# The sweep stage of a metaformer block: PE's loop over steps written out, and the late wait stated first

## The chip, the cores and the metric

One core of a Trainium2 chip runs the whole program. The metric is the device time of one execution in microseconds, median of the runs. Engines: PE (matmul; PEld is its weight load), DVE (vector), ACT (scalar), POOL (GpSimd), SP (which issues most DMAs).

## What is computed

The input is `x`, 8 images of 32 channels, 64 by 64, f32. Two blocks follow each other, each with a residual mixer and a residual mixture of experts. The first mixer is a spectral convolution. The second, which the change touches, is four dependent sweeps over the image's rows or columns:

```python
def _sweep(x, w, b, axis, reverse):
    rows = jnp.moveaxis(x, axis, 0)
    if reverse:
        rows = rows[::-1]
    def step(prev, row):
        new = row + jax.nn.relu(_conv1d(prev, w, b))
        return (new, new)
    _, rest = jax.lax.scan(step, rows[0], rows[1:])
    ...

out = _sweep(x, w_d, b_d, axis=2, reverse=False)
out = _sweep(out, w_u, b_u, axis=2, reverse=True)
out = _sweep(out, w_r, b_r, axis=3, reverse=False)
out = _sweep(out, w_l, b_l, axis=3, reverse=True)
```

`_conv1d` is a 9-tap convolution along the row with 32 channels in and out. A sweep has 64 rows, so 63 steps; four sweeps have 252 steps, and each step needs the one before it.

## The kernel before

The program is written engine by engine, with semaphores between them; each engine runs its own list in order. Ahead of the sweeps lie the first block (layer norm, spectral convolution, experts) and the second layer norm; behind them the second experts (`experts(1)`) and the store.

**A row in memory.** The partition holds 4 neighbouring pixels times 32 channels (128), the free dimension 8 images times 16 groups of pixels. The 9 taps become 3 banded matrices of 128 by 128 (`conv_sb`), one for each neighbouring group. The current row stands in `state`, in RE, a ring of 4 slots with padding at both ends.

**Three chains.** The 8 images are split in three (`CHAINS`: 3, 3 and 2), so that one chain's matmuls run while the others are with DVE. For each step and chain PE (L718) runs 3 taps times 4 column strips of 32 (`OC`), 12 matmuls of 128 rows by 32 columns over 48 or 32 values. They are f32, and each gives two recorded passes, so a step is 36 matmuls or 72 passes. They accumulate on a bias that ACT wrote into the PSUM bank beforehand (`seed`, L851; two seeds a step, for chains 0 and 1 together and for chain 2). DVE (L1111) then takes the ReLU, adds the input row and writes the new state in one operation for each chain. POOL (L392), in the fourth sweep ACT (L865), copies the finished row to the image (the archive).

**Semaphores.** `s_st` counts the states that DVE wrote, `s_seed` the seeds, `s_cv` the convolutions that PE finished, `s_arc` and `s_arl` the archived rows. PE waits ahead of each chain for the state of the last step, and ahead of chains 0 and 2 also for the seed. DVE waits ahead of each chain for `s_cv`, and once a step for the archive of four rows back, so that a state slot is free.

**Loops.** For each of the four sweeps, PE's code has three steps written out (`u` from 1 to 3 of group 0) and then a hardware loop, `pe.Fori(1, HO)`, of 15 turns with 4 steps each. The loop's waits compare with values that registers hold and that are counted up. DVE, ACT and POOL have all 252 steps written out with constants. Ahead of sweep 3 and during sweeps 2 and 4, DMAs move rows and columns between layouts (`move_rows`, L317; `move_columns`, L328).

Of the kernel before, what the change touches and what calls it, by code (L numbers as in the profile page):

```python
# [8 lines left out]
B, C, H, W = 8, 32, 64, 64  # L9
# [5 lines left out]
Q = 4  # L15
HO = H // Q
# [6 lines left out]
CHAINS = ((0, 3), (3, 6), (6, 8))  # L23
# [17 lines left out]
def build_kernel(nc, x_in, dft, wspec, conv_w, conv_b, gate_w, gate_b, w1, w2, b2, own, out):  # L41
# [5 lines left out]
    with ExitStack() as ctx:  # L47
# [3 lines left out]
        def sem(name):  # L51
            return ctx.enter_context(nc.semaphore(name))
# [63 lines left out]
        s_st, s_cv = sem("state_ready"), sem("conv_ready")  # L116
        s_seed, s_arc, s_pad = sem("bias_in_bank"), sem("row_archived"), sem("state_zeroed")
        s_bits, s_arl = sem("banks_written"), sem("last_rows_archived")
# [139 lines left out]
        def row_count(s, t):  # L258

            return 127 * (s // 2) + 63 * (s % 2) + t + 1  # L260

        def state_count(s, t, c):

            return len(CHAINS) * (row_count(s, t) - 1) + c + 1

        def seed_of(c):

            return next(i for i, (c0, c1) in enumerate(SEEDS) if c0 <= c < c1)

        def state_slot(s, u):  # L270

            return (u + 3 * (s % 2)) % 4

        def conv_bank(s, u, c):

            b0, b1 = CHAINS[c]
            c0, c1 = SEEDS[seed_of(c)]
            bank = 2 * c0 + (s + u + 1) % 2 * (c1 - c0) + c - c0
            return PS[:, bank, 0:(b1 - b0) * HO].rearrange("p (b v) -> p b v", v=HO)
# [6 lines left out]
        def row_at(image, s, q, u):  # L286

            if s % 2:
                q, u = HO - 1 - q, Q - 1 - u
            if image is XF:  # L290
                return XF[:, Q * q + u]
            if image is XW:
                return XW[:, u, :, q, :]
            return XV[:, u, :, :, q]
# [8 lines left out]
        def wait_columns(eng, j):  # L303

            share = sum(on_pool(j, i) for i in range(Q))
            eng.wait_ge(s_ph[j], 16 * (Q * len(MOVED) - share))
            eng.wait_ge(s_php[j], 16 * share)
# [102 lines left out]
        def _(pe):  # L410
# [298 lines left out]
            for s in range(4):  # L709
                def step(q, u):  # L710
                    for c, (b0, b1) in enumerate(CHAINS):
                        if c == SEEDS[seed_of(c)][0]:
                            pe.wait_ge(s_seed, len(SEEDS) * (63 * s + Q * q + u - 1) + seed_of(c) + 1)
                        pe.wait_ge(s_st, state_count(s, Q * q + u - 1, c))
                        for d in range(3):
                            prev = state[:, state_slot(s, u - 1), b0:b1, d:d + HO]
                            for o in range(0, P, OC):
                                m = pe.matmul(conv_bank(s, u, c)[o:o + OC], conv_sb[:, s, d, o:o + OC], prev,  # L718
                                              start=False, stop=(d == 2), skip_group_check=True)
                        m.then_inc(s_cv, 1)  # L720

                for u in range(1, Q):
                    step(0, u)
                with pe.Fori(1, HO) as q:
                    for u in range(Q):
                        step(q, u)

            experts(1)

# [144 lines left out]
        def _(dve):  # L874
# [216 lines left out]
            for s in range(4):  # L1091
                if s % 2 == 0:
                    if s == 0:
                        dve.wait_ge(s_pad, 1)
                        dve.wait_ge(s_fd, 16)
                    else:
                        wait_columns(dve, 0)
                    for b0, b1 in CHAINS:
                        dve.tensor_copy(state[:, 0, b0:b1, 1:1 + HO], row_at(SRC[s], s, 0, 0)[:, b0:b1, :]).then_inc(s_st, 1)
                else:  # L1100
                    dve.wait_ge(s_arc, 63 * (s - 1) + 62)

                def step(q, u):
                    r = Q * q + u
                    if s == 3 and r > Q:
                        dve.wait_ge(s_arl, r - Q)
                    elif 63 * s + r > Q:
                        dve.wait_ge(s_arc, 63 * s + r - Q)
                    for c, (b0, b1) in enumerate(CHAINS):
                        dve.wait_ge(s_cv, len(CHAINS) * (63 * s + Q * q + u - 1) + c + 1)  # L1110
                        dve.scalar_tensor_tensor(out=state[:, state_slot(s, u), b0:b1, 1:1 + HO], in0=conv_bank(s, u, c),  # L1111
                                                 scalar=0.0, in1=row_at(SRC[s], s, q, u)[:, b0:b1, :],
                                                 op0=ALU.max, op1=ALU.add).then_inc(s_st, 1)

                for r in range(1, H):
                    if s == 2 and r < Q:
                        wait_columns(dve, r)
                    step(r // Q, r % Q)
# [71 lines left out]
```

## Time and profile before

| | us |
|---|---|
| median of 3 runs | 687.14 |
| lowest and highest | 681.44, 689.34 |
| the profiled execution | 681.41 |
| its span, first to last instruction | 679.6 |
| PE busy | 589.5 (87%) |
| DVE busy | 393.8 (58%) |
| ACT busy | 318.2 (47%) |
| POOL busy | 99.3 (15%) |
| mean granted clock of TensorE | 0.935 |

All prediction sums are made against the profiled execution. The sweeps' first matmul starts 293.9 us into the span, and their last ends at about 584 us. "Released by issue" means that the engine waited for nothing that the profile shows. PE's busy time counts pipelined passes with modelled ends. Queues named "instruction" bring program code to the engines.

### The profile page before, as it was taken

What the parts mean: (1) busy time and instruction counts of PE and PEld (TensorE: products, weight loads), DVE (VectorE), ACT (ScalarE), POOL (GpSimd) and SP (SyncE); (2) the same over time, 40 slices, a digit from 0 to 9 for tenths busy, and PEclk for the clock granted to TensorE, in tenths of its full rate; (3) what the DMA queues carried; (4) which work ended last, traced back from release to release, by engine and by line L of the source; (5) the groups of instructions that cost most, each with busy time, mean ns of one, the idle gap of its engine ahead of it and who ended that gap; (6) DMA issues with size and microseconds to landing.
All of it is one profiled execution on the core that took longest, in us unless ns stands there. A gap on an engine that the chain in (4) does not pass through costs nothing.

```text
span 679.6 us, 47989 instructions
## 1 busy us (share of the span) xinstructions
PE 589.5 (87%) x21958; PEld 542.8 (80%) x21958; DVE 393.8 (58%) x1077; ACT 318.2 (47%) x842; POOL 99.3 (15%) x220
## 2 busy tenths in 40 slices
PE   8978898999979999869997899679996999965897
PEld 7978788999969869858887888568885888964783
DVE  4648896574498265624554455436663555388626
ACT  4757896533584023433443343314443666548600
POOL 4000000000110000012222222412220033620000
PEclk9989899999988799988998899969999999987979
DMA  9631770500000000000000032310000233300006
GB/s 361 256 124 64 291 270 3 215 34 1 1 1 2 18 1 0 1 3 2 0 0 2 2 78 78 78 19 1 0 0 4 44 66 65 67 9 1 2 2 247
DMA packets 54411, 41.01 MB, mean 60 GB/s; under 512 B 49350, under 2 KB 49478, under 8 KB 53126
## 3 DMA queue, kind: packets, MB, share of 16 engines
q1 hardware_dynamic: 53816, 39.29, 18.0%
q8 instruction: 46, 0.75, 0.5%
q0 software_dynamic: 384, 0.39, 0.3%
q10 hardware_dynamic: 144, 0.39, 0.2%
q14 instruction: 21, 0.17, 0.1%
HBM read 27.49 MB, written 4.19 MB: 47 GB/s over the span
## 4 chain that ended last, share of the span: by engine, by line
PE 63%; DVE 17%; ACT 6%; SPq 6%; issue 5%; DMA 1%; POOL 0%; DVEq 0%; ACTq 0%
PE PS L718 29%; PE PS L434 5%; PE PS L687 4%; SPq L328 4%; DVE RB L958 4%; PE PS L455 3%; DVE RE L1111 3%; PE PS L509 2%; SPq L317 2%; DVE sums L997 2%; PE PS L637 2%; DVE RCD L1009 2%; PE PS L584 2%; PE PS L533 2%; PE PS L540 2%
## 5 line engine op out<-in xcount | busy, mean ns | idle before, releaser
L718 PE MATMUL PS<-RE,conv_sb 128*32 128x48 f32 (+1 forms) x18144 | 248.2, 209 | 42.2 <-issue 17.0
L718 PEld LDWEIGHTS PS<-RE,conv_sb 128*32 128x32 f32 x18144 | 231.6, 114 | 58.8 <-issue 26.8
L851 ACT COPY PS<-convb_sb 128x96 f32<-128x96 f32 x504 | 106.7, 215 | 169.0 <-DVE RE L1111 161.4
L1111 DVE SCALAR_TENSOR_TENSOR RE<-PS,RCD 128x48 f32<-128x48 f32 x378 | 74.2, 203 | 68.6 <-PE PS L718 55.0
L392 POOL COPY RCD<-RE 128x128 f32<-128x128 f32 x126 | 37.0, 293 | 206.4 <-DVE RE L1111 206.4
L1111 DVE SCALAR_TENSOR_TENSOR RE<-PS,RE 128x48 f32<-128x48 f32 x189 | 39.0, 223 | 32.5 <-PE PS L718 23.5
L1111 DVE SCALAR_TENSOR_TENSOR RE<-PS,RB 128x48 f32<-128x48 f32 x189 | 37.1, 203 | 33.6 <-PE PS L718 26.6
L784 ACT COPY RB<-PS 32x256 f32<-32x256 f32 x64 | 42.5, 664 | 7.3 <-PE PS L493 6.5
L958 DVE COPY RB<-PS 32x256 f32<-32x256 f32 x64 | 42.1, 658 | 5.6 <-PE PS L493 4.8
L455 PE MATMUL PS<-warm 128*128 128x128 bf16 x468 | 38.3, 255 | 6.2 <-ACT RCD L824 3.6
L455 PEld LDWEIGHTS PS<-warm 128*128 128x128 bf16 x468 | 35.3, 117 | 7.4 <-ACT RCD L824 4.0
L509 PE MATMUL PS<-RE,RB 128*64 128x64 f32 x1024 | 32.7, 225 | 8.2 <-DVE RCD L967 4.0
L509 PEld LDWEIGHTS PS<-RE,RB 128*64 128x64 f32 x1024 | 31.5, 140 | 9.6 <-DVE RB L958 5.3
L884 DVE TENSOR_REDUCE sums<-RE 128x32 f32<-128x1024 f32 x16 | 19.4, 1218 | 33.2 <-ACT RE L756 33.2
L756 ACT ACTIVATE RE<-PS 128x1024 f32<-128x1024 f32 x16 | 16.2, 1021 | 33.6 <-PE PS L434 33.5
L385 POOL TENSOR_TENSOR RE<-RA 128x1024 f32<-128x1024 f32 x3 | 5.7, 1893 | 179.5 <-ACT RA L817 179.5
L434 PEld LDWEIGHTS PS<-dft_sb,RCD 128*128 128x128 f32 x128 | 30.5, 328 | 0.9 <-issue 0.5
L687 PE MATMUL PS<-RCD,espread 128*128 128x512 f32 x64 | 31.2, 644 | 0.0
L434 PE MATMUL PS<-dft_sb,RCD 128*128 128x128 f32 x128 | 30.8, 396 | 0.0
L745 ACT COPY RCD<-PS 128x256 f32<-128x256 f32 (+1 forms) x40 | 24.7, 692 | 11.2 <-PE PS L698 6.0
L803 ACT COPY RB<-PS 128x512 f32<-128x512 f32 (+1 forms) x24 | 16.2, 736 | 26.1 <-PE PS L540 26.1
L614 PE MATMUL PS<-proj,RA 128*128 128x192 f32 x128 | 23.4, 343 | 5.6 <-ACT RB L817 5.2
(117 smaller groups left out, 780.8 us busy)
## 6 DMA issues: line engine op xcount, KB each, us to landing
RE<-wspec SPq DMA_DIRECT2D x8, 2048.0 KB, 8.5
RA<-x_in SPq DMA_DIRECT2D x8, 512.0 KB, 7.4
RCD<-x_in SPq DMA_DIRECT2D x1, 4096.0 KB, 13.6
out<-RA SPq DMA_DIRECT2D x8, 512.0 KB, 2.7
RCD<-RB SPq DMA_DIRECT2D x48, 64.0 KB, 2.1
RE<-RCD SPq DMA_DIRECT2D x32, 80.0 KB
RE<-RCD SPq DMA_DIRECT2D x16, 64.0 KB
RCD<-RB SPq DMA_DIRECT2D x26, 32.0 KB, 1.9
```

The source lines that it names most:

```text
L328: eng.dma_start(CO[C * bl:C * bl + C, k, i, w0:w0 + Q * (v1 - v0)], XF[C * i:C * i + C, Q * v0:Q * v1, BH * bl:BH * bl + BH, :]).then_inc( ...
L392: pool.tensor_copy(o, i).then_inc(s_arc, 1)
L434: m = pe.matmul(blk(ln_slot(g), n), src, centre, start=True, stop=True)
L455: pe.matmul(PS[:, bank, 0:P], warm[:, :], warm[:, :], start=True, stop=True)
L509: m = pe.matmul(o[:, x % 2, y], XB[:, c % 2, x, 2 * y + a].rearrange("p r q b -> p (r q b)"), WR[:, c % 3, a, x, y, :], start=True, stop=True)
L687: pe.matmul(PS[:, 4 + k % 4, :], espread[:, BL * bh:BL * bh + BL, :].rearrange("p b o -> p (b o)"), rhs, start=True, stop=True).then_inc(s ...
L718: m = pe.matmul(conv_bank(s, u, c)[o:o + OC], conv_sb[:, s, d, o:o + OC], prev, start=False, stop=(d == 2), skip_group_check=True)
L745: m = act.copy(o, i)
L784: m = act.copy(o, i)
L851: act.copy(banks_of, convb_sb[:, s:s + 1].unsqueeze(2).to_broadcast([P, c1 - c0, n])).then_inc(s_seed, 1)
L958: m = dve.tensor_copy(o, i)
L1111: dve.scalar_tensor_tensor(out=state[:, state_slot(s, u), b0:b1, 1:1 + HO], in0=conv_bank(s, u, c), scalar=0.0, in1=row_at(SRC[s], s, q, u ...
```

## The change

On PE, the three steps written out and the loop of 15 turns give way to one Python loop that writes out all 63 steps of each sweep; every wait then compares with a constant. Ahead of chains 0 and 2 PE states its wait for `s_st` before that for `s_seed`. On DVE the archive's wait, which stood ahead of the step's chains, now stands behind chain 0's wait for `s_cv`. The matmuls, vector operations and DMAs are the same in number, shape and order.

```diff
--- before.py
+++ after.py
@@ -709,9 +709,9 @@
             for s in range(4):
                 def step(q, u):
                     for c, (b0, b1) in enumerate(CHAINS):
+                        pe.wait_ge(s_st, state_count(s, Q * q + u - 1, c))
                         if c == SEEDS[seed_of(c)][0]:
                             pe.wait_ge(s_seed, len(SEEDS) * (63 * s + Q * q + u - 1) + seed_of(c) + 1)
-                        pe.wait_ge(s_st, state_count(s, Q * q + u - 1, c))
                         for d in range(3):
                             prev = state[:, state_slot(s, u - 1), b0:b1, d:d + HO]
                             for o in range(0, P, OC):
@@ -719,11 +719,8 @@
                                               start=False, stop=(d == 2), skip_group_check=True)
                         m.then_inc(s_cv, 1)
 
-                for u in range(1, Q):
-                    step(0, u)
-                with pe.Fori(1, HO) as q:
-                    for u in range(Q):
-                        step(q, u)
+                for r in range(1, H):
+                    step(r // Q, r % Q)
 
             experts(1)
 
@@ -1101,13 +1098,13 @@
                     dve.wait_ge(s_arc, 63 * (s - 1) + 62)
 
                 def step(q, u):
-                    r = Q * q + u
-                    if s == 3 and r > Q:
-                        dve.wait_ge(s_arl, r - Q)
-                    elif 63 * s + r > Q:
-                        dve.wait_ge(s_arc, 63 * s + r - Q)
                     for c, (b0, b1) in enumerate(CHAINS):
-                        dve.wait_ge(s_cv, len(CHAINS) * (63 * s + Q * q + u - 1) + c + 1)
+                        r = Q * q + u
+                        dve.wait_ge(s_cv, len(CHAINS) * (63 * s + r - 1) + c + 1)
+                        if c == 0 and s == 3 and r > Q:
+                            dve.wait_ge(s_arl, r - Q)
+                        elif c == 0 and 63 * s + r > Q:
+                            dve.wait_ge(s_arc, 63 * s + r - Q)
                         dve.scalar_tensor_tensor(out=state[:, state_slot(s, u), b0:b1, 1:1 + HO], in0=conv_bank(s, u, c),
                                                  scalar=0.0, in1=row_at(SRC[s], s, q, u)[:, b0:b1, :],
                                                  op0=ALU.max, op1=ALU.add).then_inc(s_st, 1)
```

## Rows read from the trace of the kernel before

**Rows 1.** The page's part 1: busy us, share of the span, instructions.

```profile
PE 589.5 (87%) x21958; PEld 542.8 (80%) x21958; DVE 393.8 (58%) x1077; ACT 318.2 (47%) x842; POOL 99.3 (15%) x220
```

**Rows 2.** The page's part 5: busy, mean ns, then idle before and releaser.

```profile
L718 PE MATMUL PS<-RE,conv_sb 128*32 128x48 f32 (+1 forms) x18144 | 248.2, 209 | 42.2 <-issue 17.0
```

**Rows 3.** Stretches: length, then busy us and instructions by engine, clock, DMA share.

```profile
365.80:378.30 12.50, 8.23 (x471) 7.33 (x460) 4.09 (x21) 2.71 (x13) 1.76 (x6) 0.68 0.02 5
378.30:436.30 58.00, 53.69 (x4032) 50.32 (x4032) 32.97 (x169) 23.72 (x113) 16.42 (x56) 0.98 0.23 57
526.20:584.20 58.00, 53.37 (x4032) 49.66 (x4032) 33.12 (x169) 36.09 (x166) 15.48 (x6) 1.00 0.35 59
sum 290.30, PE 248.17 PEld 231.63 DVE 150.75 ACT 120.72 POOL 74.95; mean PE 31.02 PEld 28.95 DVE 18.84 ACT 15.09 POOL 9.37
```

**Rows 4.** Time line: start, length, group, idle before it; DVE's sweep operations.

```profile
344.57 0.66 DVE L1111 SCALAR_TENSOR_TENSOR RE<-PS,RCD 128x48 f32<-128x48 f32 x3 [0.25 <-PE PS L718]
345.85 0.66 DVE L1111 SCALAR_TENSOR_TENSOR RE<-PS,RCD 128x48 f32<-128x48 f32 x3 [0.63 <-PE PS L718]
346.74 0.66 DVE L1111 SCALAR_TENSOR_TENSOR RE<-PS,RCD 128x48 f32<-128x48 f32 x3 [0.23 <-PE PS L718]
```

**Rows 5.** Chain of waits in order of time: start, length, what.

```profile
344.50 0.02 DVEq L1110
```

**Rows 6.** Time line, PE alone, start of sweep 1.

```profile
298.14 1.90 PE L718 MATMUL PS<-RE,conv_sb 128*32 128x32 f32 x124 [1.68 <-issue]
302.18 2.45 PE L718 MATMUL PS<-RE,conv_sb 128*32 128x48 f32 x123 [2.14 <-issue]
306.15 1.19 PE L718 MATMUL PS<-RE,conv_sb 128*32 128x48 f32 x55 [1.53 <-issue]
```

**Rows 7.** Time line, PE alone, start of sweep 2.

```profile
369.49 2.42 PE L718 MATMUL PS<-RE,conv_sb 128*32 128x32 f32 x123 [1.61 <-issue]
373.12 2.45 PE L718 MATMUL PS<-RE,conv_sb 128*32 128x48 f32 x124 [1.20 <-issue]
376.80 5.91 PE L718 MATMUL PS<-RE,conv_sb 128*32 128x48 f32 x349 [1.23 <-issue]
```

**Rows 8.** Time line, PE alone, start of sweep 3.

```profile
441.91 1.51 PE L718 MATMUL PS<-RE,conv_sb 128*32 128x48 f32 x72 [6.01 <-DVE RE L1099]
450.71 2.23 PE L718 MATMUL PS<-RE,conv_sb 128*32 128x48 f32 x123 [0.70 <-issue]
454.62 1.05 PE L718 MATMUL PS<-RE,conv_sb 128*32 128x48 f32 x68 [1.68 <-issue]
```

**Rows 9.** Time line, PE alone, start of sweep 4.

```profile
517.39 1.98 PE L718 MATMUL PS<-RE,conv_sb 128*32 128x48 f32 x124 [1.61 <-issue]
521.19 1.84 PE L718 MATMUL PS<-RE,conv_sb 128*32 128x48 f32 x124 [1.82 <-issue]
524.86 1.24 PE L718 MATMUL PS<-RE,conv_sb 128*32 128x32 f32 x73 [1.82 <-issue]
```

**Rows 10.** Queues (packets, MB, share): whole span; 366 to 379 us; 319 to 366 us.

```profile
q8 instruction: 46, 0.75, 0.5%
...
q8 instruction: 4, 0.07, 2.0%
...
q14 instruction: 3, 0.02, 0.2%
```

**Rows 11.** Stretches: half clock in sweep 1, the mix, a burst in sweep 4.

```profile
306.15:312.10 5.95, 5.78 (x311) 5.65 (x314) 2.44 (x12) 1.72 (x8) 1.09 (x4) 0.50 0.01 3
72.20:78.70 6.50, 4.59 (x127) 4.38 (x127) 6.23 (x10) 5.99 (x10) 0.00 (x0) 1.00 0.66 277
536.20:546.80 10.60, 9.78 (x744) 9.12 (x743) 6.17 (x33) 6.64 (x32) 0.00 (x0) 1.00 0.59 99
```

**Rows 12.** Time line, PE alone, in the spectral mix.

```profile
72.24 0.94 PE L493 MATMUL PS<-dft_sb,RA 128*128 128x128 f32 x7 [0.92 <-issue]
78.76 0.45 PE L509 MATMUL PS<-RE,RB 128*64 128x64 f32 x8 [1.93 <-issue]
```

## The prediction

> **What bounds the kernel now.** I read the page's busy shares first. PE works 87% of a span of 679.6 us, and 18,144 of its 21,958 recorded passes are one line, L718, the three-chain sweep [rows 1, 2]. Then I cut the sweeps' 290.3 us (293.9 to 584.2) into stretches [rows 3]. They fall into two kinds. Each sweep begins with code that runs once (three peeled steps, then the first turn of the loop, 7 steps or 504 passes), and goes on with 14 more turns of the same loop code (56 steps, 4,032 passes). The repeated part takes 58.0 us for 56 steps in sweep 2, 1.04 us a step. Sweep 2's first-run part takes 12.5 us for 7 steps, 1.79 us a step, for the same matmuls. What the unrolled program will resemble is this first-run part, because all its code is run once. So the question is what makes it slow.
>
> In the repeated part, the time line shows DVE's bursts of three at 344.57, 345.85 and 346.74 [rows 4]: a step of 1.28 us over the turn of the loop, and one of 0.89 us within it, where PE is nearly full (72 passes). With 0.9 us for a plain step, the turn costs 0.38 us. In the chain of waits, DVE's queue stands at L1110 at 344.50, 0.02 us long, and DVE's operation begins at 344.57 [rows 4, 5]: the wait for PE, stated last of two, is taken as an instruction of its own and costs some 0.06 us.
>
> In the first-run parts PE stops for 0.70 to 2.14 us with the releaser "issue", which means that nothing the profile shows was awaited: no semaphore, no data [rows 6 to 9]. Between two such stops stand 123 or 124 passes each time. A pass is two instructions (weight load and matmul), so that is 248 instructions and a few waits and register operations. The queue that carries code fits this exactly. Queue q8 moved 46 packets, 0.75 MB, 16 KB each [rows 10]. Counting each sweep's loop body once, PE's program has (21,958 - 18,144 + 4 x 7 x 72) x 2 = 11,660 instructions and a few waits, 253 or more a packet: 64 bytes each, a packet being a page of 256. Around the first-run part of sweep 2, from 366 to 379 us, q8 moves 4 packets, and in the 47 us of repeated loop from 319 to 366 us none at all, only another engine's q14 appears [rows 10]. So loops run from code already on the chip, and straight code is fetched page by page, each page arriving when the previous one has long been used up.
>
> **The page period.** From resumption to resumption the seven intervals are 4.04 and 3.97 (sweep 1), 3.63 and 3.68 (sweep 2), 3.91 (sweep 3), 3.80 and 3.67 us (sweep 4) [rows 6 to 9]; mean 3.81. In each of them PE needs 1.8 to 2.5 us from first to last pass and then starves. That it starves three times running, without the gap shrinking, says that the fetch is one page ahead only and does not build up a lead. Four packets in 13 us is of the same size.
>
> **The change, part by part.**
> (a) Removed: 60 loop turns, with their register operations and branches. In the loop regime this would save 60 x 0.38 = 22.8 us [rows 4]. Under a page period of 3.81 us it saves nothing, for a page's own work is far shorter: 256 instructions at 146 a step are 1.75 steps, 1.6 us at 0.9 us a step. Even at a granted clock of 0.50 (the lower level, 1.2 GHz), where 311 passes or 4.3 steps take 5.95 us [rows 11], it is 1.75 x 1.38 = 2.4 us. So the clock, which was 0.68 in the starved stretch of sweep 2 [rows 3], doesn't enter the sum.
> (b) Added: straight code. A step is 72 passes x 2 = 144 instructions and two extra waits (two of the three chains have two waits, of which one needs its own instruction), 146. 252 steps x 146 / 256 = 143.7 pages. At 3.81 us: 547.5 us. Bounds: 3.63 gives 521.6, 4.04 gives 580.5.
> (c) Columns at the start of sweep 3: PE waited 6.01 us for the first state [rows 8], and then briefly for the next columns. A fetch under way there covers some of it; a page's period at most (3.8), half of it on average: + 5 us with the later waits (0 to 7).
> (d) Transfers in the sweeps. Sweeps 2 and 4 have bursts of rows and columns being moved; the DMA share is 0.23 and 0.35 over the 58 us of repeated loop [rows 3], and 0.59 within the burst from 536.2 [rows 11]. So the bursts run (0.23 + 0.35) x 58 / 0.59 = 57 us in all; their work stays the same. No page was fetched in them, so the price is not shown. The nearest row is the spectral mix, where the DMA share is 0.66 and PE resumes after "issue" at 72.24 and 78.76: a period of 6.52 us [rows 11, 12], of which its own passes take 4.6. At 6.52 us the bursts hold 57 / 6.52 = 9 pages, each 2.7 us late, 24 us; at the quiet period it is 0. I take 12, the middle, as the share is near the mix's but the code before the stop was slower there.
> (e) The DVE's late wait first: 0.02 + 0.04 us less before DVE's first chain, at most 0.06 x 60 turns = 4 us on today's path (within a turn PE is the bound), and 0 behind a page fetch. The same holds for PE's swapped order of `s_st` and `s_seed`: mostly, both semaphores are up when the page comes. Bounds: 0 to -4.
> (f) Everything outside the sweeps: unchanged, 0 (up to 2 more if the next stage starts at half clock).
>
> Sum: 547.5 + 5 + 12 = 564.5 us in place of 290.3, + 274. The profiled execution took 681.41 us (span 679.6), so 681.4 + 274 = **955 us**. That execution is at the fast end of the three runs (681.44 to 689.34, median 687.14), and an after held by fetches should scatter no less; I leave 955. By the bounds: 681.4 + (521.6 - 290.3) - 4 = 909, and 681.4 + (580.5 + 7 + 24 - 290.3) + 2 = 1,005.
>
> A rule speaks against this. The Trainium skill (Runtime: NRT & Kernel Launch, section "Instruction fetch mechanics") says that the sequencer streams straight code by itself, that crossing a 16 KiB boundary is mostly hidden, and that kernels prefer full unrolling over branches. The trace disagrees: thirteen crossings cost 0.70 to 2.14 us each [rows 6 to 9, 12].
>
> **The rivals.**
> 1. Faster. The stops are a start-up matter, of the first pages after a loop, and once straight code runs on, the fetch keeps up. Place: each 256-instruction boundary in L718. Price: the turns go (-22.8), the late waits too (-4), and if the first-run parts fall to 7 x 0.9 = 6.3 us as well, 6.2 in each of four sweeps (-25): 630 to 659 us, about 650. It decides once the page period is under 1.75 x 1.04 = 1.8 us. For it: crossings elsewhere go unnoticed. Against: those codes take over 4 us a page by themselves, with 128-column matmuls, and the same stop appears in the mix at 72.24 and 78.76, which no loop precedes [rows 12]. 0.06. The skill's rule above would give this outcome.
> 2. No change. Two pages in flight, a period of half 3.81: 143.7 x 1.91 = 274 us and the columns' 5, 670 to 690 us. Against: q8 shows one packet per period. 0.02.
> 3. Slower, by less. The period measured is partly that of pages entered behind a loop or beside the profiler, and runs at about 3.0 us: 143.7 x 3.0 = 431, 681.4 + 431 + 17 - 290.3 = 839; 760 to 905. 0.10.
> 4. Slower still. The small packets of the moves hold back fetches more than in the mix, or the quiet period is over 4.04: over 1,010 us. 0.10.
> 5. The change doesn't do what it says, because the builder keeps a loop: excluded, the steps are written out one by one.
>
> **The numbers.** My forecast (909 to 1,005) has 0.72, rivals 1 to 4 0.06, 0.02, 0.10 and 0.10. Predicted time 955 us, range 895 to 1,015: the forecast's own 0.72 and the near edges of rivals 3 and 4, together some 0.8. A measurement of this kernel can tell about 1% from no change. Faster by over 1% 0.06, within 1% 0.02, slower 0.92.
>
> **What would show it.** q8 should move 46 + (252 x 146 - 4 x 1,036) / 256 = 173 packets, about 2.8 MB, spread evenly over the sweeps, 3.6 to 4.1 us apart (1,036 is a sweep's code now). The waits should show L718 "issue" as the largest entry, some 140 times, with runs of 123 to 125 passes between. PE's busy share should fall to about 0.6 or less, the sweeps' slices to tenths of 4 to 6. DVE's bursts should come in irregular steps, mean 2.2 us, and its wait at L1110 should leave the chain. My prediction is wrong if the pages arrive closer than 3 us (then the lead does build up), or if DVE or PE at half clock rather than "issue" ends most stops. The share of (d) shows as a longer period inside the bursts.

## The result and the profile after

The changed kernel takes 946.78 us (median of 4 runs, 942.8 to 952.64) beside 688.0 us before: a ratio of 1.380, 95% interval 1.369 to 1.391. That is slower by 259 us, with 955 us forecast and a range of 895 to 1,015. The profiled execution took 950.65 us (span 948.8), 269.2 us more than that of before; the sum had said 274. The kernel before has shorter and longer executions (676 to 693 us in all groups), and every ratio compares the shorter ones of both kernels, so that it can differ from the quotient of the medians.

The page of the changed kernel, parts 1 and 2 (busy time and share; tenths of busy time in 40 slices of 23.7 us), the code queue of part 3, and PE's sweep line of part 5:

```profile
PE 651.4 (69%) x21958; PEld 598.8 (63%) x21958; DVE 399.7 (42%) x1077; ACT 315.8 (33%) x842; POOL 100.4 (11%) x220
...
PE   8888899979996565555454655556555544569698
...
PEclk9999999998996856867868557775766889759758
...
q8 instruction: 174, 2.85, 1.3%
...
L718 PE MATMUL PS<-RE,conv_sb 128*32 128x48 f32 (+1 forms) x18144 | 305.5, 240 | 252.4 <-issue 245.8
```

These answer to [rows 1, 2, 10]. The number of passes is the same. Their idle time went from 42.2 to 252.4 us, and 245.8 us of it has the releaser "issue" (17.0 before). The code queue moved 174 packets in place of 46; 173 had been worked out. The middle slices, all of the sweeps, are half busy.

PE's waits over the whole span (engine, line, releaser, us in total, times, longest):

```profile
PE PS L718 <- issue: 245.8, 141, 2.8
```

That is one stop a page: 141 for 143.7 pages. And the time line of PE in sweep 1 (start, length, passes, idle time before):

```profile
307.21 2.56 PE L718 MATMUL PS<-RE,conv_sb 128*32 128x48 f32 x126 [1.15 <-issue]
310.71 2.59 PE L718 MATMUL PS<-RE,conv_sb 128*32 128x32 f32 x127 [0.95 <-issue]
314.67 1.59 PE L718 MATMUL PS<-RE,conv_sb 128*32 128x48 f32 x126 [1.38 <-issue]
318.58 1.66 PE L718 MATMUL PS<-RE,conv_sb 128*32 128x48 f32 x126 [2.31 <-issue]
322.18 1.58 PE L718 MATMUL PS<-RE,conv_sb 128*32 128x48 f32 x126 [1.95 <-issue]
326.11 1.66 PE L718 MATMUL PS<-RE,conv_sb 128*32 128x32 f32 x127 [2.34 <-issue]
```

It is the pattern of [rows 6 to 9], now without end: 126 or 127 passes, then a stop (123 to 125 had been expected; with the few waits between them they make 256 instructions). Read the starts, not the lengths. A page's work takes 1.6 us or 2.6 us, and the stop before the next page is mostly the shorter, the longer the work was, so that the starts stand 3.50 to 3.96 us apart all the same. A cost that came with each page would be added to its work; a period covers the work.

What the period is made of can be read from the code queue between two such starts, 318.58 and 322.18 (40 slices of 0.09 us; a packet's bytes stand in the slice in which it starts):

```profile
GB/s 0 0 0 0 0 0 0 0 0 0 0 0 182 0 0 0 0 0 0 0 0 0 0 0 0 0 0 0 0 0 0 0 0 0 0 0 0 0 0 0
q8 instruction: 1, 0.02, 1.8%
```

The one packet starts at 319.71, 1.1 us after PE has entered the page, ends at 320.78, and PE enters the next page 1.4 us behind that. The trace has it so in every one of the 139 periods of the sweeps that can be cut out: one packet, starting 1.34 us (mean; 1.06 to 2.25) after PE enters a page, 1.15 us long, and the next page entered 1.39 us (1.19 to 1.61) after its end. So a page is asked for when PE enters the one before it, and not earlier: that is what "one page ahead" means here.

By stretch (length, then busy us and instructions of PE, PEld, DVE, ACT and POOL, granted clock, DMA share, GB/s), one line for each sweep:

```profile
291.40:423.00 131.60, 76.52 (x4495) 71.09 (x4495) 37.93 (x187) 26.69 (x128) 18.19 (x62) 0.69 0.02 5
423.00:565.00 142.00, 77.01 (x4545) 71.61 (x4545) 38.33 (x189) 26.43 (x126) 18.48 (x63) 0.69 0.12 30
565.00:707.00 142.00, 78.69 (x4544) 72.96 (x4545) 42.15 (x193) 26.11 (x126) 22.51 (x70) 0.68 0.04 8
707.00:849.50 142.50, 73.24 (x4560) 67.99 (x4559) 38.59 (x191) 40.08 (x186) 17.28 (x7) 0.75 0.18 30
sum 558.10, PE 305.45 PEld 283.65 DVE 157.00 ACT 119.31 POOL 76.46; mean PE 76.36 PEld 70.91 DVE 39.25 ACT 29.83 POOL 19.11
```

The sweeps take 558.1 us in place of 290.3, so 267.8 of the 269.2 us are theirs. The part ahead of them is 2.5 us shorter (291.4 in place of 293.9), the part behind them 3.9 us longer.

### The profile page after: what moved, and what is told of

It is laid out like the page before. It is cut to its first block, busy times and chain, and to the rows that moved or that the text cites. A ratio compares the mean times of both kernels' runs of the same rounds, so it can differ in the third digit from the quotient of the medians.

```text
span 948.8 us, 47145 instructions
## 1 busy us (share of the span) xinstructions
PE 651.4 (69%) x21958; PEld 598.8 (63%) x21958; DVE 399.7 (42%) x1077; ACT 315.8 (33%) x842; POOL 100.4 (11%) x220
## 4 chain that ended last, share of the span: by engine, by line
PE 56%; issue 27%; DVE 12%; ACT 3%; SPq 1%; POOL 1%; DMA 0%; ACTq 0%
PE PS L718 32%; PE PS L434 4%; PE PS L687 3%; DVE RB L955 3%; PE PS L637 2%; DVE sums L994 2%; DVE RCD L1006 2%; PE PS L584 2%; PE PS L533 1%; PE PS L455 1%; PE PS L540 1%; PE PS L614 1%; PE PS L509 1%; PE PS L554 1%; DVE RCD L1029 1%
## 5 line engine op out<-in xcount | busy, mean ns | idle before, releaser
L718 PE MATMUL PS<-RE,conv_sb 128*32 128x48 f32 (+1 forms) x18144 | 305.5, 240 | 252.4 <-issue 245.8
L718 PEld LDWEIGHTS PS<-RE,conv_sb 128*32 128x32 f32 x18144 | 283.7, 139 | 274.3 <-issue 267.7
L1108 DVE SCALAR_TENSOR_TENSOR RE<-PS,RCD 128x48 f32<-128x48 f32 x378 | 76.7, 203 | 199.5 <-PE PS L718 185.6
L1108 DVE SCALAR_TENSOR_TENSOR RE<-PS,RE 128x48 f32<-128x48 f32 x189 | 41.6, 223 | 95.8 <-PE PS L718 85.6
L1108 DVE SCALAR_TENSOR_TENSOR RE<-PS,RB 128x48 f32<-128x48 f32 x189 | 38.3, 203 | 102.7 <-PE PS L718 95.6
L881 DVE TENSOR_REDUCE sums<-RE 128x32 f32<-128x1024 f32 x16 | 19.4, 1218 | 34.0 <-ACT RE L753 34.0
L392 POOL COPY RB<-RE 128x128 f32<-128x128 f32 x63 | 18.5, 293 | 118.5 <-DVE RE L1108 118.5
L334 POOL TENSOR_TENSOR RA<-RCD 128x1024 f32<-128x1024 f32 x6 | 17.0, 2853 | 106.2 <-DMA RCD<-RB 106.2
L994 DVE TENSOR_REDUCE sums<-RE 128x32 f32<-128x1024 f32 x16 | 19.4, 1213 | 16.1 <-ACT RE L812 11.0
```

The lines of the kernel that those rows point to most:

```text
L392: pool.tensor_copy(o, i).then_inc(s_arc, 1)
L994: dve.tensor_reduce(sums[:, 32 * g:32 * g + 32], square[:, g % 2, 0:1024].rearrange("p (a c) -> p a c", c=C), AX_X, ALU.add).then_inc(s_su ...
```

## The experiments

Theory: straight code reaches PE in pages of 256 instructions, one page ahead, one every 3.8 us or so; code of a loop stays on the chip. The rivals: the waits (their order, or constants in place of registers), the granted clock, a fixed cost a page or a step, and the size of what stays on the chip. The kernel before ran beside all of them; its median was 683.0 to 687.8 us in the three groups. Where no ratio stands, medians are compared.

**The order of the waits alone.**

```diff
 PE, in the loop, which stays
-                        if c == SEEDS[seed_of(c)][0]:
-                            pe.wait_ge(s_seed, ...)
                         pe.wait_ge(s_st, state_count(s, Q * q + u - 1, c))
+                        if c == SEEDS[seed_of(c)][0]:
+                            pe.wait_ge(s_seed, ...)
 DVE: as in the change
```

> The kernel before with the order of the two waits changed on PE and DVE and nothing else; PE keeps its loop. Theory (code pages: a page of 256 instructions arrives every 3.87 us, one ahead, and only straight code pays): no page is added, so 684 to 688 us beside a before of 688: a gain of at most 60 turns x 0.06 = 4 us. Rival (the slowdown comes from the way the waits are taken): a visible part of the 259 us shows here, over 700.

Measured: 686.87 us beside 686.4, ratio 1.013 (1.007 to 1.019). The medians are level and the ratio lies on the slow side: the swap brings nothing, and costs two hundredths at most (13 us by the interval). By this run it has at most a twentieth of the 259 us. The chain of waits in the repeated part of sweep 1, of this kernel:

```profile
341.45 3.47 PE PS L718 x264
344.92 0.02 issue
344.94 0.22 DVE RE L1111
345.17 0.02 issue
345.19 0.25 ACT PS L851
345.44 0.02 issue
345.46 3.45 PE PS L718 x264
```

DVE's queue at L1110 [rows 5] is out of the chain, as the change meant, but a turn of the loop still takes 4.01 us (341.45 to 345.46), against 4.04 at the same place before (341.22 to 345.26). At most 0.03 of the 0.06 us show.

**The unrolling alone.**

```diff
 PE, waits in their old order; DVE as before
-                for u in range(1, Q):
-                    step(0, u)
-                with pe.Fori(1, HO) as q:
-                    for u in range(Q):
-                        step(q, u)
+                for r in range(1, H):
+                    step(r // Q, r % Q)
```

> The kernel before with PE's sweep program written out over 63 steps a sweep, waits in their old order on both engines. Page theory: 940 to 955, as with the whole change, 174 packets on the code queue and some 140 stops with the releaser issue. Rival (wait order matters in straight code): differs from 947 by over 10 us, to either side.

Measured: 941.79 us beside 686.4, ratio 1.388 (1.380 to 1.397). Its code queue and PE's wait at L718:

```profile
q8 instruction: 174, 2.85, 1.3%
...
PE PS L718 <- issue: 207.1, 139, 2.6
```

The whole loss is the unrolling's: its 255 us are the 259 of the whole change, within the scatter of runs. This profile also speaks against the granted clock as the cause. The mean clock was 0.750 here and 0.795 in the changed kernel, and PE was busy for 682.1 us in place of 651.4. Yet the execution was not longer (944.20 us, against 950.65), because the stops are shorter in sum, 207.1 us in place of 245.8.

**More steps in a loop turn.** Three sizes of the loop's body, each with all 63 steps of a sweep:

```diff
 12 steps a turn (20: the same with 5 in place of 3, and 3 turns)
-                with pe.Fori(1, HO) as q:
-                    for u in range(Q):
-                        step(q, u)
+                with pe.Fori(0, 5) as g:
+                    for j in range(3):
+                        for u in range(Q):
+                            step(3 * g + (j + 1), u)
 8 steps a turn
-                for u in range(1, Q):
-                    step(0, u)
-                with pe.Fori(1, HO) as q:
-                    for u in range(Q):
-                        step(q, u)
+                for r in range(1, 8):
+                    step(r // Q, r % Q)
+                with pe.Fori(1, 8) as g:
+                    for j in range(2):
+                        for u in range(Q):
+                            step(2 * g + j, u)
```

> The kernel before with 12 steps in a loop turn and 5 turns, in place of 4 steps and 15 turns. The loop's code is 12 x 150 = 1,800 instructions, 7.0 pages. Page theory, if the chip holds 7 pages: first-run code grows from 7 to 15 steps a sweep, 4.7 pages x 4 sweeps x (3.87 - 1.8) = + 39 us, 40 turns fewer are - 15 us: about 712 us, with 46 + 4 x 4.7 = 65 code packets. Rival (nothing but the branch counts, straight code is free): 688 - 15 = 673. Rival (what is held is smaller than 7 pages): every turn is fetched anew, 930 or more and 170 or more packets.

> The kernel before with 20 steps in a loop turn and 3 turns; the loop's code is 20 x 150 = 3,000 instructions, 11.7 pages. Page theory with a store of less than 11 pages on the chip: all of it is fetched in each turn, 940 to 990 us and 170 or more code packets, although there is a loop. If the store holds it: first-run code is 23 steps a sweep, 9.4 pages more x 4 x 2.07 = + 78, turns - 18: about 748 us with 84 packets.

> The kernel before with 7 steps written out and then 7 loop turns of 8 steps; the loop's code is some 1,197 instructions, 4.7 pages. Page theory with a store of about 8 pages on the chip (a turn of 7.0 pages was held in one sweep and fetched anew in another): this one is always held. First-run code is 15 steps a sweep, 8.7 pages in place of 4.1: 4.6 x 4 x (3.81 - 1.8) = + 37 us, 32 turns fewer - 12: about 713 us, 64 code packets. Rival (what is held is below 4.7 pages): 900 or more and over 150 packets. Rival (straight code costs nothing, turns do): 676.

Measured: 12 steps 923.48 us beside 686.4; 20 steps 999.77 beside 686.4, ratio 1.476 (1.468 to 1.484); 8 steps 713.23 beside 683.03, ratio 1.052 (1.044 to 1.061). The code queue tells them apart. With 20 steps a turn, over the whole span and from 393 to 440 us, about one turn:

```profile
q8 instruction: 189, 3.10, 1.3%
...
q8 instruction: 13, 0.21, 1.9%
```

A body of 11.7 pages is fetched anew in each turn, loop or no loop, and costs even more than straight code. With 12 steps a turn, the whole span, then 425 to 456 us (one turn of sweep 2), then 338 to 361 us (two turns of sweep 1):

```profile
q8 instruction: 155, 2.54, 1.2%
...
q8 instruction: 8, 0.13, 1.7%
...
q14 instruction: 2, 0.02, 0.2%
```

The same 7.0 pages were held in three turns of sweep 1 and fetched anew in every turn of sweep 2. By my expectation it should have been one or the other throughout. Over the four sweeps, six of the 16 repeated turns ran without a stop, three each in sweeps 1 and 4, and ten were fetched anew. The time line of PE in sweep 4 shows one turn of each kind, one behind the other:

```profile
769.09 11.28 PE L718 MATMUL PS<-RE,conv_sb 128*32 128x48 f32 x864 [0.47 <-ACT PS L852]
785.67 1.97 PE L718 MATMUL PS<-RE,conv_sb 128*32 128x48 f32 x93 [5.30 <-issue]
788.85 2.45 PE L718 MATMUL PS<-RE,conv_sb 128*32 128x48 f32 x123 [1.21 <-issue]
```

A held turn is 864 passes without a stop; a missed one begins with a stop of 5.30 us here (3.82 at 429.22, in sweep 2), which I take for the price of a branch to code that isn't there, and goes on page by page. So 7.0 pages are on the edge. What decides between the two, these runs don't show. With 8 steps a turn, 4.7 pages, the whole span, and then 291 to 320 us:

```profile
q8 instruction: 65, 1.06, 0.6%
...
q8 instruction: 8, 0.13, 1.9%
```

From 320 to 353 us no packet of q8 appears at all, in 2,280 passes. And the time is 30 us over the kernel before, where 25 had been worked out: the turns saved are less than the first-run code added. (That the 713 us came out to the microsecond is luck, as the kernel before was 5 us quicker in this group.) The Trainium skill (Runtime: NRT & Kernel Launch, section "Instruction fetch mechanics") gives PE an instruction store of 128 KiB, 2,048 instructions, which is 8 pages. The three runs agree in size, with 4.7 pages held and 11.7 not; but the 7.0 pages, which are under 8, were missed in most turns.

**Fewer instructions for the same arithmetic.** A strip of 64 or 128 columns halves or quarters the code of a step:

```diff
-OC = P // 4
+OC = P // 2      (or P)
```

> The kernel before with two column strips of 64 per tap in place of four of 32: 72 instructions a step in place of 144, same arithmetic. In the mix a pass of 64 columns and 64 values takes 3.95 us / 128 = 31 ns, so 48 values some 23 ns and a step 36 x 23 ns = 0.83 us, near the 0.9 of now. Page theory: the first-run code of a sweep falls from 4.1 to 2.2 pages, whose own work is then as long as a fetch, so some 4 x 6 = 24 us go: about 664 (645 to 690). Rival (strips of 64 make PE slower than the code saves): over 690.

> The changed kernel (all steps written out) with strips of 64: 74 instructions a step, 72.8 pages. Page theory: 72.8 x 3.87 = 282 us for the sweeps, 5 for the columns, so 681 + 287 - 290 = 678 (665 to 700), and the code queue falls from 174 to 103 packets, with a period of still some 3.9 us for 256 instructions. Rival (straight steps cost 2.2 us each by their waits or by the clock, not by their bytes): still about 945. Rival (a gap per page, not a period: 1.7 us a page whatever the page's own work): 252 x 0.9 + 72.8 x 1.7 = 351, so 742.

Measured: with the loop 668.44 us beside 687.81, ratio 0.974 (0.959 to 0.990); unrolled 694.24 beside 687.81. Queues of the unrolled kernel, whole span and 300 to 420 us; its sweeps; PE's waits in them; two stops in its PE time line; and the sweeps of its partner with the loop:

```profile
q8 instruction: 103, 1.69, 1.0%
...
q8 instruction: 31, 0.51, 1.9%
...
295.00:588.00 293.00, 276.67 (x9070) 272.08 (x9070) 157.11 (x757) 121.86 (x564) 74.84 (x202) 0.98 0.15 30
...
PE PS L718 <- issue: 6.3, 19, 0.6
...
392.92 3.85 PE L718 MATMUL PS<-RE,conv_sb 128*64 128x48 f32 x124 [0.58 <-issue]
397.42 2.77 PE L718 MATMUL PS<-RE,conv_sb 128*64 128x48 f32 x88 [0.65 <-issue]
```

```profile
291.00:572.00 281.00, 274.51 (x9072) 273.43 (x9068) 157.01 (x758) 121.75 (x563) 74.31 (x202) 0.98 0.14 28
...
341.08 0.21 DVE L1111 SCALAR_TENSOR_TENSOR RE<-PS,RCD 128x48 f32<-128x48 f32 x1 [0.24 <-PE PS L718]
342.13 0.81 DVE L1111 SCALAR_TENSOR_TENSOR RE<-PS,RCD 128x48 f32<-128x48 f32 x3 [0.24 <-PE PS L718]
343.29 0.81 DVE L1111 SCALAR_TENSOR_TENSOR RE<-PS,RCD 128x48 f32<-128x48 f32 x3 [0.35 <-PE PS L718]
```

This is the run that weighs most. 31 pages in 120 us are 3.87 us a page, again. But a page now holds 3.46 steps (256 / 74) of 1.05 us (341.08 to 342.13, in the partner), 3.63 us of work, so little is left of the stops, 6.3 us in all, and the same 252 steps written out take 293 us. A cost a step of 2.2 us would have given 945, a gap of 1.7 us a page 252 x 1.05 + 72.8 x 1.7 = 388 us for the sweeps. Both rivals are out. The four executions took 682 to 695 us, 4 to 17 over the 678 expected. In the profiled one, of 693.63 us, 6 of these lie in the sweeps (293 against 287): I take it that with a step of 1.05 us in place of the 0.83 expected the page's work comes so near to the period that their scatter adds up. The loop's partner is 12 us shorter in the sweeps (281 against 293), and its turn costs 0.11 us (342.13 to 343.29 is 1.16) in place of 0.38.

> The kernel before with one strip of 128 columns a tap: 36 instructions a step. 9 passes of 128 values took 1.27 us, so 48 values some 53 to 60 ns, 18 passes 1.0 to 1.1 us a step: 252 x 1.1 + 23 for the turns = 300 us against 290, 690 to 760 in all. Both theories say the same here; it is the partner of the next.

> The changed kernel with one strip of 128: 38 instructions a step, 37.4 pages, a page holding 6.7 steps or 7 us of work, more than a fetch. Page theory: no stop is left, and writing the steps out gains what the turns cost: 10 to 25 us under its partner with the loop. Rival (a gap per page): 37.4 x 1.7 = 64 us more, so 40 above it. Rival (a cost per straight step): far above it.

Measured: 1,360.21 us with the loop (ratio 1.985, 1.958 to 2.012), 1,361.73 unrolled (1.993, 1.963 to 2.023). No stop, as the theory says: unrolled, PE is busy for 955.2 of 960 us, and a fixed gap of 1.7 us a page would have cost 64 us, against the 1.5 between the two. The queue moves 4 packets of q8 from 320 to 420 us, one in 26 us: the fetch goes at PE's pace where PE is the slower.

```profile
300.00:1260.00 960.00, 955.20 (x4479) 955.06 (x4478) 155.40 (x750) 120.80 (x558) 75.89 (x201) 0.50 0.04 9
```

The expected gain over the loop is absent as well: with a pass every 960 / 4,479 = 214 ns, PE hides a turn altogether. My size for the pass, 53 to 60 ns, was wrong by a factor of four. It came from passes of 128 values at full clock and assumed that the time goes with the values; and the clock was 0.50 in this stretch.

**Strips mixed.**

```diff
 in the three written-out steps (f_mixB)
-                    step(0, u)
+                    step(0, u, 2 * OC)
 ... (`step` takes the strip's width as its third argument)
 and in each turn's first step besides (f_mixA)
-                        step(q, u)
+                        step(q, u, 2 * OC if u == 0 else OC)
```

> The kernel before with strips of 64 columns in the three written-out steps of each sweep only; the loop keeps strips of 32. Code falls by 216 instructions or 0.84 pages a sweep. Page theory: - 0.84 x 3.81 + 3 x 0.16 = - 2.7 us a sweep, 11 in all: 677. Rival (first-run code costs for another reason, such as the clock or the banks): 688.

> As the last, and strips of 64 also in the first step of each loop turn, where PE's sequencer has the turn's register operations and branch to do besides. Page theory: 0.28 pages a sweep less, 4 us in all; and a step of 1.28 us over the turn becomes some 1.15, 60 x 0.13 = 8 us: 665.

> Strips of 64 throughout and the loop kept, again, beside the last two: 668. It has the shortest code and plain steps of 1.05 us; the mixed one has plain steps of 0.91.

Measured beside 683.03 us: wide strips in the written-out steps 682.78, ratio 0.990 (0.983 to 0.997), level medians and a ratio that says 7 of the 11 us expected, with 43 packets of q8 in place of 46; in the turn's first step too 692.56 (665 expected), ratio 1.008 (1.001 to 1.014), a miss; wide strips throughout 672.46, ratio 0.985 (0.980 to 0.989). DVE's time line in the miss:

```profile
342.64 0.66 DVE L1111 SCALAR_TENSOR_TENSOR RE<-PS,RCD 128x48 f32<-128x48 f32 x3 [0.25 <-PE PS L718]
344.04 0.81 DVE L1111 SCALAR_TENSOR_TENSOR RE<-PS,RCD 128x48 f32<-128x48 f32 x3 [0.74 <-PE PS L718]
345.15 0.66 DVE L1111 SCALAR_TENSOR_TENSOR RE<-PS,RCD 128x48 f32<-128x48 f32 x3 [0.29 <-PE PS L718]
```

The step over the turn is 1.40 us, not 1.15, and the next 1.11, not 0.91. So the turn's cost, here 0.35 us over a wide step of 1.05, is not hidden by fewer instructions in the step behind it. Why it shrinks to 0.11 when all steps are wide I can only suppose: PE is then behind its sequencer when the turn comes. No run tests that. Wide strips throughout with the loop kept is the fastest version found, 668.44 and 672.46 us in two groups.

## Why the prediction was right, by its own steps

**The period.** Seven intervals of the kernel before gave 3.81 us. In the changed kernel, taking the starts of each 256th instruction, the 108 intervals without a transfer beside them have a mean of 3.81 us (3.40 to 4.25), and the 32 beside one 4.05. That the means agree to a hundredth is luck: the seven intervals of the kernel with the order of the waits alone have a mean of 4.06, by which term (b) would have been 36 us larger. Rival 1 (the fetch catches up) would have needed 1.8 us, rival 2 half of 3.81, rival 3 3.0, and rival 4 over 4.04 in the quiet: all out.

**(a), (b).** 143.7 pages were expected and 174 - 46 = 128 more packets came; 127.5 were worked out. The clock doesn't enter, as (a) said: two stretches of sweep 1 of the changed kernel, four and seven page periods long, one at each clock level:

```profile
314.67:329.92 15.25, 6.49 (x506) 5.97 (x507) 4.26 (x21) 2.83 (x14) 2.06 (x7) 1.00 0.02 5
333.55:359.90 26.35, 17.71 (x884) 16.50 (x884) 7.30 (x36) 5.17 (x24) 3.52 (x12) 0.50 0.02 4
```

3.81 us a page at 2.4 GHz, 3.76 at 1.2 GHz. PE was busy for 6.5 us of the first and 17.7 of the second; the page takes its time.

**(c), (d).** The columns' wait stayed: in sweep 3 PE waited 4.0 us behind DVE at L1096 and 2.1 more behind L1108 (6.01 us stood before the first state in the kernel before [rows 8]), near the 5. The transfers cost 32 x (4.05 - 3.81) = 8 us in place of 12, and in the kernel with the unrolling alone, counted the same way, 33 x (3.82 - 3.78), 1 us. The price of 6.52 us from the mix was far too high a bound. Sum for the sweeps: 547.5 + 5 + 12 = 564.5 against 558.1, 6.4 too much, 4 of it in (d).

**(e).** 0 to -4: nothing was found, and perhaps a small loss.

**(f).** This term was too small. Everything behind the sweeps (849.5 to the end, before from 584.2) takes 99.3 us in place of 95.4:

```profile
849.50:948.80 99.30, 83.08 (x760) 69.78 (x760) 55.34 (x69) 40.43 (x45) 10.67 (x9) 0.79 0.15 49
```

```profile
584.20:679.60 95.40, 75.36 (x760) 62.03 (x760) 55.23 (x70) 40.43 (x45) 11.01 (x10) 0.87 0.17 54
```

The same 760 passes run at a granted clock of 0.79 in place of 0.87. 3.9 us where I had allowed 2. That the half-idle sweeps are to blame fits the two rows, but no run shows it by itself. With the 2.5 us gained ahead of the sweeps, the parts outside come to +1.4 where the sum had 0, so the total was only 5 us off (274 against 269.2): the two errors partly cancel. And PE's busy share fell to 0.69, not to 0.6: the sweeps' passes count 305.5 us in place of 248.2, at a granted clock of 0.68 to 0.75 by sweep.

What the text had less right: that each page arrives "when the previous one has long been used up". The stop varies from 0.95 to 2.34 us in the six rows above, while the starts stay 3.50 to 3.96 us apart. And loops "run from code already on the chip" was seen for bodies of up to 4.7 pages, and at 7.0 pages only in some turns.

## What to carry to other kernels

Before a loop is written out, count what its code needs: instructions a step, divided by 256, times the page period that the profile shows at the straight code nearest to it, here 3.8 us. Compare that with the time in which the engine works through a page. Where the work is longer (128-column passes here), straight code is free; where it is shorter (32-column passes, 1.6 us a page), a loop that fits on the chip is worth far more than its turns cost (259 us against 23 here), and fewer, larger instructions help (strips of 64: 947 to 694 us written out, 688 to 668 with the loop). Stops with the releaser "issue" at equal numbers of instructions are the sign to look for.

## What was not expected of the hardware

- A loop body of 7.0 pages was held in one turn and missed in the next (769.09 and 785.67 above), and a miss at the branch came with a stop of 5.30 us.
- With strips of 128 columns PE was busy for 99.5% of 960 us, and the granted clock was 0.50 all the while; with strips of 64, busy for 98%, it was 0.98. A pass took 214 ns against 29 (1.05 us / 36), of which the clock explains a factor of two at most and the doubled columns another, if the time goes with the columns loaded. The rest, and why the clock stayed low under an engine that never rested, these runs don't explain.
- Two loops that differ only in strip width pay 0.38 and 0.11 us a turn.
